# Attention's projection products within a batch, issued in two parts over two steps

## The reference

```python
# x: layernorm of the running x; key = value = context (4, 512, 512)
Q = (query @ Wq).reshape(b, q_len, 4, 4, 32) / sqrt(32)
K = (key @ Wk).reshape(b, kv_len, 4, 32)
V = (value @ Wv).reshape(b, kv_len, 4, 32)
scores = einsum('bqghd,bkgd->bghqk', Q, K) + slope * (k_pos - q_pos)
w = softmax(where(mask, scores, lowest))
out = einsum('bghqk,bkgd->bqghd', w, V)
x = x + tanh(g) * (out.reshape(b, q_len, 512) @ Wo)
```

## Time and profile before

| | |
|---|---|
| median of 3 runs | 1145.18 us (1138.4 to 1151.26) |
| the profiled execution's own time | 1142.93 us |
| its span, first to last instruction | 1141.1 us |
| PE busy | 997.2 us (87%) |
| DVE, ACT, POOL busy | 727.6, 587.4, 410.0 us |
| mean granted TensorE clock | 0.949 of full speed |

### The profile page before, as it was taken

One profiled execution on the slowest core, in us unless ns is written; L12 is line 12 of the kernel. 1 busy time (PEld: TensorE's weight loads), 2 busy tenths in 40 slices (PEclk: granted clock), 3 DMA queues, 4 the chain that ended last, 5 costly groups with the idle time before them and its releaser, 6 DMA issues. The chain is left out here.

```text
span 1141.1 us, 17357 instructions
## 1 busy us (share of the span) xinstructions
PE 997.2 (87%) x5411; PEld 448.9 (39%) x5412; DVE 727.6 (64%) x1438; ACT 587.4 (51%) x882; POOL 410.0 (36%) x467
## 2 busy tenths in 40 slices
PE   0465889999779999999999995999899999999936
PEld 0342445555423223323332322544345555556402
DVE  6989978888787676587478757576242434333218
ACT  6897989999337676476467562423221111111100
POOL 1100335544410252235133433007407887910460
PEclk9988889999979999999999997999899999999967
DMA  8322920000633334214211044977426998657763
GB/s 325 117 74 97 343 94 1 1 1 1 137 95 85 99 76 117 71 49 90 70 58 44 12 117 128 229 277 268 158 91 137 229 212 216 170 145 156 264 185 148
DMA packets 189633, 148.03 MB, mean 130 GB/s; under 512 B 132804, under 2 KB 151876, under 8 KB 189048
## 3 DMA queue, kind: packets, MB, share of 16 engines
q1 hardware_dynamic: 180616, 118.07, 37.9%
q0 software_dynamic: 8080, 27.60, 7.4%
q10 hardware_dynamic: 864, 1.44, 0.4%
HBM read 73.03 MB, written 44.02 MB: 103 GB/s over the span
## 5 line engine op out<-in xcount | busy, mean ns | idle before, releaser
L1709 DVE CUSTOM_DVE_ANT_0 ajunk<-p_row,mask_row 128x512 bf16<-128x512 f32 x256 | 166.1, 686 | 60.8 <-PE p_row L1555 58.9
L1472 ACT ACTIVATE early_place<-p_col,mask_col,any_key 128x512 f32<-128x512 f32 x128 | 92.9, 776 | 63.5 <-PE p_col L1606 63.1
L1472 ACT ACTIVATE prob<-p_col,mask_col,any_key 128x512 f32<-128x512 f32 x128 | 93.5, 786 | 38.5 <-PE p_col L1606 38.0
L1555 PE MATMUL p_row<-ks,early_place 99*128 99x512 f16 x256 | 100.3, 394 | 8.7 <-DVE top L1709 7.9
L1362 POOL TENSOR_TENSOR o<-sum_a,rec 32x512 f32<-32x512 f32 x30 | 39.3, 1310 | 187.6 <-DMA rec<-inv_d 185.5
L1606 PE MATMUL p_col<-early_place,ks 101*128 101x512 f16 x256 | 97.7, 385 | 1.2 <-ACT early_place L1472 0.6
L2883 DVE SCALAR_TENSOR_TENSOR shid<-s_up,ssilu 128x352 f32<-128x352 f32 x36 | 18.9, 525 | 99.3 <-PE s_up L2788 99.3
L2803 PE MATMUL s_down<-mw,shT 128*128 (+5 forms) x396 | 75.8, 379 | 0.0
L2717 ACT ACTIVATE ssilu<-s_gate 128x352 f32<-128x352 f32 x36 | 16.7, 463 | 108.4 <-PE s_gate L2788 108.4
L1568 PE MATMUL p_out<-prob,v 128*64 128x512 f32 x256 | 69.0, 618 | 0.1
L1568 PE MATMUL p_out<-early_place,v 128*64 128x512 f32 x256 | 69.0, 618 | 0.0
(11 more groups left out here) (408 smaller groups left out, 2107.7 us busy)
## 6 DMA issues: line engine op xcount, KB each, us to landing
x_slots<-nought SPq DMA_DIRECT2D x3, 3072.0 KB, 17.7
y_slots<-spare SPq DMA_DIRECT2D x36, 256.0 KB, 2.4
early_place<-in_ctx SPq DMA_DIRECT2D x8, 1024.0 KB, 6.1
early_place<-halves_d SPq DMA_DIRECT2D x45, 128.0 KB, 2.4
halves_d<-halves SPq DMA_DIRECT2D x18, 256.0 KB, 2.1
x<-in_x SPq DMA_DIRECT2D x4, 1024.0 KB, 7.3
w<-in_L_ffn_w SPq DMA_DIRECT2D x1, 4096.0 KB, 18.0
w<-in_L_ffn_w SPq DMA_DIRECT2D x4, 1024.0 KB, 4.7
```

The lines of the kernel that those rows point to most:

```text
L1472: nc.scalar.activation(prob[s % 4][:, c, :], p_col[c][:], ACT.Exp, bias=mask_col[:, b, k:k + 1], scale=any_key[:, b:b + 1]).then_inc(t_exp, 1)
L1555: nc.tensor.matmul(p_row[n % 2][:], qs[0:ROWS_R, j, g, t * P:(t + 1) * P], ks[b % 2][0:ROWS_R, g, :], start=True, stop=True).then_inc(t_ro ...
L1709: nc.vector.tensor_tensor_reduce(junk[:, n % 2, :], p_row[n % 2][:], mask_row[:, blk // HPG, :], 1.0, -3e38, ALU.add, ALU.max, top[blk % 2 ...
```

## The change

Fills of kind `k`, `v`, `q` and `y` that stand inside a batch at a step above 0 are split. Step s issues the second half of its own split fills (or the whole of the others), and then the first half of the split fills of step s + 1. A half is the first or last six of 12 products, or two of the four row tiles of `v`. The wait for the bank stands before the first half. The wait for `t_xt` stands before each half of q0; that for `t_ol` asks for two blocks before y0's first half, for all four before its second. The semaphore that tells of the finished fill is raised after the second half. q1 goes from step 17 to step 18. The helper `part` is renamed `piece`.

```diff
         self.at, self.step, self.kind, self.n, self.batch = at, step, kind, n, batch
+        self.split = 0 <= at < B and step > 0 and kind != "top"
...
-    NEXT = {6: ("k", 0), 8: ("v", 0), 12: ("q", 0), 17: ("q", 1), 24: ("q", 2)}
+    NEXT = {6: ("k", 0), 8: ("v", 0), 12: ("q", 0), 18: ("q", 1), 24: ("q", 2)}
...
-            def three(out_, lhs, rhs, n):
-                for i in range(n):
+            def three(out_, lhs, rhs, n, part=None):
+                for i in range(n) if part is None else range(part * n // 2, (part + 1) * n // 2):
...
-            def fill_(f):
+            def fill_(f, part=None):
                 p = p_fill[f.i % 2]
-                if f.i >= 2:
+                if f.i >= 2 and part != 1:
                     g = FILLS[f.i - 2]
                     pe.wait_ge(*((t_topc, g.n + 1) if g.kind == "top" else (t_free, g.free + 1)))
...
-                    for t in range(TPB):
+                    for t in range(TPB) if part is None else range(part * TPB // 2, (part + 1) * TPB // 2):
...
                     if f.n == 0:
-                        pe.wait_ge(t_ol, HPG * (f.batch + 1))
-                        if f.batch == 0:
+                        pe.wait_ge(t_ol, HPG * f.batch + (HPG // 2 if part == 0 else HPG))
+                        if f.batch == 0 and part != 1:
                             pe.wait_ge(t_split, 1 + KB)
...
-                mm.then_inc(t_fill, 1)
+                if part != 0:
+                    mm.then_inc(t_fill, 1)
...
                     for f in fills_at(b, s):
-                        fill_(f)
+                        fill_(f, 1 if f.split else None)
+                    for f in fills_at(b, s + 1):
+                        if f.split:
+                            fill_(f, 0)
```

More of the change, by code:

```diff
@@ L1057, in stage_attention, with piece @@
     wl = sb(st, "wl", [P, KB * 2 * D], F16)
-    def part(t, at, k, n, c0, c1):
+    def piece(t, at, k, n, c0, c1):
         return t[:, at + k * n + c0:at + k * n + c1]
@@ L1523, in fill_ @@
                     pe.wait_ge(t_ct, 16 * TPB * (f.batch + 1))
-                    mm = three(p[:], lambda k, h: kv[:, h, k * KV:(k + 1) * KV], lambda k, h: ctxT[:, h, k, :], KB)
+                    mm = three(p[:], lambda k, h: kv[:, h, k * KV:(k + 1) * KV], lambda k, h: ctxT[:, h, k, :], KB, part)
                 elif f.kind == "v":
-                    for t in range(TPB):
+                    for t in range(TPB) if part is None else range(part * TPB // 2, (part + 1) * TPB // 2):
                         mm = three(p[:, t * KV:(t + 1) * KV], lambda k, h: ctxT[:, h, k, t * P:(t + 1) * P],
@@ L1533, in fill_ @@
                             pe.wait_ge(t_split, KB)
-                    mm = three(p[:], lambda k, h: part(W[h], Q0, k, D, f.n * P, (f.n + 1) * P), lambda k, h: xT[:, h, k, :], KB)
+                    mm = three(p[:], lambda k, h: piece(W[h], Q0, k, D, f.n * P, (f.n + 1) * P), lambda k, h: xT[:, h, k, :], KB, part)
                 else:
                     if f.n == 0:
-                        pe.wait_ge(t_ol, HPG * (f.batch + 1))
-                        if f.batch == 0:
+                        pe.wait_ge(t_ol, HPG * f.batch + (HPG // 2 if part == 0 else HPG))
+                        if f.batch == 0 and part != 1:
                             pe.wait_ge(t_split, 1 + KB)
-                    mm = three(p[:], lambda j, h: oT[h][:, j, f.n * P:(f.n + 1) * P], lambda j, h: part(W[h], O0, j, D, 0, D), HPG)
-                mm.then_inc(t_fill, 1)
+                    mm = three(p[:], lambda j, h: oT[h][:, j, f.n * P:(f.n + 1) * P], lambda j, h: piece(W[h], O0, j, D, 0, D), HPG, part)
+                if part != 0:
+                    mm.then_inc(t_fill, 1)
             def row_scores(blk, t, g):
@@ L1582, in _ @@
                 for hs, hm in passes:
-                    mm = nc.tensor.matmul(p_fill[f.i % 2][:], part(W[hs], Q0, t, D, f.n * P, (f.n + 1) * P), xT[:, hm, t, :],
+                    mm = nc.tensor.matmul(p_fill[f.i % 2][:], piece(W[hs], Q0, t, D, f.n * P, (f.n + 1) * P), xT[:, hm, t, :],
                                           start=(t == 0 and hs + hm == 0), stop=(t == KB - 1 and hs == 1))
@@ L1612, in _ @@
                     for f in fills_at(b, s):
-                        fill_(f)
+                        fill_(f, 1 if f.split else None)
+                    for f in fills_at(b, s + 1):
+                        if f.split:
+                            fill_(f, 0)
             def result(f, j, parts):
                 for hs, hm in parts:
-                    mm = nc.tensor.matmul(bank(f)[:], oT[hs][:, j, f.n * P:(f.n + 1) * P], part(W[hm], O0, j, D, 0, D),
+                    mm = nc.tensor.matmul(bank(f)[:], oT[hs][:, j, f.n * P:(f.n + 1) * P], piece(W[hm], O0, j, D, 0, D),
                                           start=(j == 0 and hs + hm == 0), stop=(j == HPG - 1 and hs == 1))
```

## The result

The changed kernel took 1159.9 us in the median of six runs (1147.66 to 1160.66), the kernel before 1146.59 us in six of its own timed beside it (1138.4 to 1158.08): a ratio of 1.0109, with a 95% interval from 1.007 to 1.0148. Ratios, and means of the two kernels, leave out slow executions, those more than 1.5% above the fastest of the same kernel; here that is the one of 1158.08. Weighted by their widths the three give 1.0070, or 8.0 us slower. The profiled execution of the changed kernel took 1147.66 us, with a span of 1145.9.

The account below looks back on a forecast made before the run. PE's own issue was taken as the bound. Waits for the turned rows (3.5) and the bank (3.8), all else 0, gave +7.3 us on the profiled 1142.93, 1150.2, and 1152 as median; range 1144 to 1161.

Parts of the forecast that it names:

- The bound and the size of the relief: In the attention loop PE's own issue is the bound; smoothing could win at most 6.4 us, gain taken 0.
- The first rival, smoothing: DVE and ACT absorb the new waits and PE's pauses vanish: 1139 at best, half of it 1142 to 1146; chance 0.15.
- The wait for the turned rows: End of step 11, batches 0 to 2: PE waits for q0's fourth transpose, 3.5 us in all, bounds 2.5 to 6.6.
- The wait for the bank: End of step 13, batches 1 and 2: y0's first half waits 1.9 us each for q0's bank, 3.8 in all.
- q1's step: Moving q1 from step 17 to 18 delays SP's copy and the top rows: cost 0, at most 1 us in three batches.
- the other guards: Banks for first halves of k, v, q0, y1, y2, q1, y3, q2 are free, y0's `t_ol` asks less: cost 0.
- the split itself: Two groups of six products cost the same as one of 12: 0, at most 5.9 us over 27 split fills.
- the third rival (SP's queue): q1's move makes the top rows late at step 24, 1 to 2 us in three batches: 1156 to 1158; chance 0.08.
- The clock: Loop waits of 0.9 to 1.9 us, below a 2.02 us pause that halved the clock, leave it full: cost 0.
- the second rival: Half clock follows each of five waits, 1.7 us lost for each or twice that: 1161 to 1169; chance 0.12.
- The sum: Loop waits of 3.5 and 3.8 make +7.3 us, nothing later hides it: 1152, 0.6% more; chance 0.64.
- slower by over 1%: Whole-kernel outcome given 0.21: the clock's fall 0.12, and 0.09 for a median that scatter carries over 1%.

Follow-up runs that it names:

- the three: The changed kernel timed three times beside the kernel before, with nothing else altered: ratios 1.0109, 1.0045 and 1.0068.
- the two variants without the new waits: The changed kernel with q0 and y0 left whole, ratio 0.9984; the changed kernel with the top fill first and q0 whole, ratio 1.0009.
- experiment 5: Kernel before, fills whole, q3 and q2 moved to steps 2 and 26: ratio 1.0053; to 1 (batch 0 stays at 0) and 25: 0.999, 0.9973.
- Experiment 3: Changed kernel with the top fill ahead of q0 and y0 in the list: ratio 1.0005; separately, with q1 back at step 17: 1.0079.
- experiment 4: Changed kernel with the top fill first in the list and q0 whole, every other fill still split: ratio 1.0009.

## Why the prediction held, step by step

**The bound and the size of the relief.** PE's issue is the bound, and splitting relieved next to nothing: 317.57 and 317.62 us for the two variants without the new waits, against 316.55. Without the unsteady step 1 of batch 0 they are 0.1 more and 0.5 less than before. The reason given holds. The old pauses stand behind q3 (not split) and in steps 26 and 27, behind the second half of q2, where DVE is no better off than with a whole q2. In the changed kernel their sum went from 3.1 us to 2.5 only. What the prediction did not list is the pause in step 1 of batch 0, 0.6 us before and the largest of them. The first rival, smoothing, falls. PE does wait at the ends of steps 11 and 13. What moved the pauses was moving whole fills to them (experiment 5), not halves away from other places.

**The wait for the turned rows.** The sum took 1.2, 0.9 and 1.4 us, 3.5 in all; the steps lengthened by 1.16, 1.43 and 1.33 beyond a plain step with one half fill (3.29), 3.9 in all. Batches 0 and 2 are within 0.1. Batch 1 was too small by 0.5, and DVE's timeline in step 8 of the changed kernel shows why:
```profile
441.39 1.53 DVE L1770 TENSOR_TENSOR keep<-xn,keep 128x512 f16<-128x512 f32 x1
442.85 0.68 DVE L1674 SCALAR_TENSOR_TENSOR halves<-p_fill,halves 128x512 f16<-128x512 f32 x1
443.50 0.69 DVE L1715 CUSTOM_DVE_ANT_0 ajunk<-p_row,mask_row 128x512 bf16<-128x512 f32 x1
...
444.11 0.69 DVE L1715 CUSTOM_DVE_ANT_0 ajunk<-p_row,mask_row 128x512 bf16<-128x512 f32 x1
...
444.72 1.28 DVE L1770 TENSOR_TENSOR keep<-xn,keep 128x512 f16<-128x512 f32 x1
```
Step 8 starts at 442.75, so its first maximum comes 0.75 us later, as the sum had it (0.74). The fourth low half of the rows starts 1.55 us after its old start of 443.17. PE itself runs 1.12 us later than before by then (453.47 - 1.37 = 452.10 against 450.98). So the delay that counts is 0.43 where 0.5 had been taken. But the instruction takes 1.28 us instead of 0.96, another 0.32. 0.4 + 0.43 + 0.32 = 1.15. The fourth transpose is issued at 450.1 and lands after 3.2 us, as before, at 453.3: 1.2 us after PE is ready, and PE starts some 0.15 after that. The mis-sized part is thus one duration, which I had carried over as fixed although the same group ranges from 0.69 to 1.35 us in the earlier trace rows.

What sets that duration stands on POOL, first in the kernel before, then in the changed one:
```profile
442.30 1.27 POOL L1362 TENSOR_TENSOR o<-sum_b,rec 32x512 f32<-32x512 f32 x1
...
444.19 1.26 POOL L1363 TENSOR_TENSOR o<-sum_a,rec 32x512 f32<-32x512 f32 x1
```
In both, POOL is in a TENSOR_TENSOR of its own when DVE's begins, and DVE's ends 0.56 us (444.13) and 0.55 us (446.00) after POOL's. With q0 alone split that batch's wait is 0.66.

**The wait for the bank.** Predicted 1.9 twice, ended by DVE's low half. Measured in three profiles of the changed kernel: 1.85 us of idle time before y0's first product, twice in each, ended by just that; where the clock stays at full the step takes 5.20 us, 1.9 more than a plain one with one half fill. Experiment 3 shows that the list's order causes it. That ACT's chain comes no earlier holds too: ACT still waits for PE's transpose.

**q1's step, the other guards, the split itself.** All taken as 0. q1 at 17 or 18 makes no difference to the loop, so the third rival (SP's queue) falls for this change: in batch 0 the top rows are issued from 395.94, 2.5 us later than in the earlier trace rows, and step 24 starts at 400.85 with no wait. No other fill shows a wait. The 5.9 us upper end for 27 switches is excluded by experiment 4.

**The clock.** Taken as 0, and here the forecast was a little short: one of the two waits for the bank in the first profile was followed by half clock. Step 13 took 1.2 and step 14 0.5 us more for it, 1.7 us, just what the second rival had given as the price of one. That rival wanted it five times, and over three profiles it came once in fifteen waits. The prediction names a granted clock below 1.00 in the loop as a sign that it is wrong; in this one term the first profile, at 0.99, shows that sign. The means show no more half clock than before. The condition I used, "below 2.02 us it stays at full", is not a threshold: 1.85 us is enough at times (see the last section). As for the section "A second HAM failure mode: psum-queue depth-cycling" of the Trainium skill's page "TensorE: Matmul & The Clock Gate", the traces hardly bear it out for this loop: with five waits between groups of products and the same cycling through banks, the granted clock was 1.00 over 324.69 and 324.56 us, and fell once in the first measurement's profile.

**The sum.** Forecast +7.3; the loop shows +8.1 and +8.0 without the fall of the clock and +9.2 with it. Out of these 8.1 and 8.0, 3.8 is the bank and 4.1 and 4.2 the turned rows, which leaves 0.2 and 0.0 for all the rest (step 1 of batch 0 is 0.6 and 0.4 longer, the other steps together 0.3 to 0.4 shorter). The forecast time of 1152 was built on the median of 1145.18. The two later measurements gave 1153.0 and 1151.63, the first 1159.9. The 6 to 8 us more that its executions ran at half clock are worth some 3 to 4 of these; why they did, when the kernel was the same, is open, and so is the remainder. Taken alone, this measurement falls into the case "slower by over 1%" that the prediction gave 0.21, and 1159.9 lies in its range only because the range was drawn up to 1161 for the clock's case and for scatter. I read its ratio together with the two others, and the mean of the three, 1.0070, is close to the forecast 0.6%. The profiled execution itself hides about half of its loss of 9.2 us: from DVE's last sum into x to the end of the span it took 437.7 us where the profile before has 442.2, a difference that the other two profiles of the same kernel (446.0 and 444.7) don't show.

## What to carry to other kernels

A fill moved one step ahead wants all that it waits for one step sooner. So look up, for each guard, what the guarded product waits for now and how much slack is left at the new place: here two guards out of nine kinds of fill had none (a bank two places back in the list, a DMA's landing), and they cost the whole 8 us. Where the bound engine's pauses are known by step, move work to the step where the pause is; smoothing elsewhere is worth nothing. And when a whole time scatters by more than the effect, measure the stretch that the change touches (here 0.1 us from one profile to the next of the same kernel, against 6 to 17 between whole executions), and look at its single steps: one pause ahead of the change differed by up to 1.5 us between kernels that are the same up to there.

## What the runs showed of the hardware

- A TENSOR_TENSOR of DVE that begins while POOL is in one of its own ends 0.55 to 0.58 us after POOL's. This holds for all 48 such instructions (`keep<-xn,keep`) in the loops of the 14 profiles. 46 of them took 0.96 to 1.72 us. The 120 that began with POOL idle took 0.63 or 0.69, also where POOL's began behind them.
- The same pause does not always have the same effect on the clock. Ten pauses of PE of 1.85 us, at the same place of the program, were followed by 3.4 us at half clock in two cases (once in the changed kernel, once with y0 alone) and by none in eight. None of the eighteen pauses of 0.6 to 1.6 us at step 11 in six profiles was.
- One chip ran both kernels 30 us faster: 1114.81 us in the median for the kernel before, where it had 1144 to 1148 in the other measurements. The loop was as long there (313.25 against 313.34 for the kernel with q3 at 1 and q2 at 25), so attention is not the cause. In these two profiles all of it lies after attention, 409.2 against 444.4 us. The kernel before shows 85 us at half clock in the mean on that chip where the others had 112 to 117. That accounts for some 15 us; what the other 15 are stays open. The ratio of the two kernels was 0.9973 there and 0.999 elsewhere, the same within its interval.
